# Reordering two steps: the eighth gelu and the state's high part on ScalarE, the fourth piece of the second feed-forward product and the second tile's products with the state on TensorE

## The reference, cut to what matters

```python
x = x + attention(layernorm(x))
x = x + ffn(layernorm(x))

# attention: xn is the normalized x, xx its difference to the token before
xk, xv, xr, xg = (xn + xx * maa for maa in (maa_k, maa_v, maa_r, maa_g))
r, k, v = xr @ Wr.T, xk @ Wk.T, xv @ Wv.T      # split by head
g = silu(xg @ Wg.T)
# in order over chunks of 64 tokens, for each head:
att = (r_c @ k_c) * w_mat                       # 64 x 64 weights
y_c = att @ v_c + (r_c @ state) * wb
state = ws * state + (k_c * wk) @ v_c
# then
out = (groupnorm_by_head(y) * gamma + beta) * g @ Wo.T

# ffn
D = gelu(fp16(xn2) @ W0.T + bias0)
E = fp16(D) @ W1.T + bias1
```

## Time and profile before

| what | value |
|---|---|
| median of 3 runs | 2086.19 us (2080.97 to 2089.77) |
| profiled execution, its own time | 2082.99 us |
| span of its trace | 2081.2 us |
| granted TensorE clock, mean | 0.995 of full speed |
| TensorE matmul busy | 96% of the span |
| VectorE busy | 84% |
| ScalarE busy | 62% |
| GpSimd busy | 16% |
| DMA, mean share of the 16 engines | 76% for the dynamic queue |

### The profile page before, as it was taken

One profiled execution on the slowest core, in us unless ns is written; L12 is line 12 of the kernel. 1 busy time (PEld: TensorE's weight loads), 2 busy tenths in 40 slices (PEclk: granted clock), 3 DMA queues, 4 the chain that ended last, 5 costly groups with the idle time before them and its releaser, 6 DMA issues.

```text
span 2081.2 us, 64752 instructions
## 1 busy us (share of the span) xinstructions
PE 2002.4 (96%) x27206; PEld 1421.4 (68%) x27206; DVE 1743.3 (84%) x3687; ACT 1294.1 (62%) x2081; POOL 333.1 (16%) x329
## 2 busy tenths in 40 slices
PE   5888999999999999999999999999999999999999
PEld 5767667677667667766666766666776676677666
DVE  7778889888889888888988888888888898888761
ACT  7866556666556576656667665656765666766452
POOL 1011111111111111111111111111111111111110
PEclk8999999999999999999999999999999999999999
DMA  6877677887777788777778877778887777887767
GB/s 213 203 199 211 199 224 230 241 248 217 216 231 222 233 249 239 206 223 230 221 239 249 226 209 221 224 229 249 243 219 214 229 226 236 245 243 199 215 236 264
DMA packets 428979, 471.97 MB, mean 227 GB/s; under 512 B 259600, under 2 KB 309392, under 8 KB 428688
## 3 DMA queue, kind: packets, MB, share of 16 engines
q1 hardware_dynamic: 427056, 467.64, 76.1%
q10 hardware_dynamic: 1632, 0.18, 0.1%
HBM read 316.21 MB, written 25.17 MB: 164 GB/s over the span
## 4 chain that ended last, share of the span: by engine, by line
PE 78%; SPq 5%; ACT 5%; DVE 4%; DMA 4%; issue 2%; POOL 0%; ACTq 0%; DVEq 0%
PE F L1132 18%; PE F L1068 16%; PE B L879 9%; PE B L1040 8%; PE sc L879 7%; PE YT L911 5%; PE YT L879 3%; PE YT L963 2%; DMA y<-ygT 2%; ACT hT L1766 2%; SPq L2025 2%; PE YT L982 2%; PE YT L1012 1%; PE sc L941 1%; PE F L836 1%
## 5 line engine op out<-in xcount | busy, mean ns | idle before, releaser
L1132 PE MATMUL F<-ring,hT 128*128 128x512 f16 x1984 | 468.0, 379 | 19.3 <-ACT hT L1766 18.8
L1068 PE MATMUL F<-xT,ring 128*128 128x256 f16 x3840 | 449.3, 273 | 5.6 <-ACT hT L1766 3.7
L1068 PEld LDWEIGHTS F<-xT,ring 128*128 128x128 f16 x3840 | 369.9, 98 | 65.3 <-issue 8.2
L1132 PEld LDWEIGHTS F<-ring,hT 128*128 128x128 f16 x1984 | 186.7, 98 | 224.9 <-ACT hT L1766 33.5
L879 PE MATMUL B<-mix,WT 128*128 128x256 f16 x2304 | 267.5, 273 | 0.3 <-DVE gT L1371 0.3
L1766 ACT ACTIVATE hT<-F,b,f_rho 128x256 f16<-128x256 f32 x480 | 244.0, 561 | 37.8 <-PE F L1068 37.8
L879 PEld LDWEIGHTS B<-mix,WT 128*128 128x128 f16 x2304 | 222.6, 98 | 33.6 <-DVE gT L1371 0.7
L276 DVE SCALAR_TENSOR_TENSOR mixf<-dx,maa,xnT 128x256 f32<-128x256 f32 x512 | 238.6, 527 | 0.1
L1969 POOL TENSOR_TENSOR Shl<-S,Shl 128x256 f16<-128x256 f32 x128 | 104.6, 817 | 723.3 <-ACT Shl L1723 723.3
L1717 ACT ACTIVATE att<-att 128x512 f16<-128x512 f32 x256 | 147.5, 624 | 110.3 <-DVE att L1332 110.3
L1723 ACT ACTIVATE Shl<-S 128x256 f16<-128x256 f32 x128 | 53.1, 415 | 224.1 <-PE YT L982 201.9
(11 more groups left out here) (196 smaller groups left out, 2993.5 us busy)
## 6 DMA issues: line engine op xcount, KB each, us to landing
ring<-w_dram SPq DMA_DIRECT2D x512, 512.0 KB, 4.7
kx<-kT SPq DMA_DIRECT2D x96, 256.0 KB, 3.7
rx<-rT SPq DMA_DIRECT2D x96, 256.0 KB, 4.3
xa<-in_L_attn_x SPq DMA_DIRECT2D x32, 512.0 KB, 7.7
vbd<-vN SPq DMA_DIRECT2D x256, 64.0 KB
x<-in_L_attn_x SPq DMA_DIRECT2D x32, 512.0 KB, 6.0
out<-x SPq DMA_DIRECT2D x31, 512.0 KB, 3.9
w_dram<-ring SPq DMA_DIRECT2D x20, 256.0 KB, 3.2
```

The costliest lines, as they stand in the source:

```text
L1068: mm = eng.matmul(up_place(f, j)[:, i * BT:(i + 1) * BT], ring[:, use % RING, i, a * C + kk * P:a * C + (kk + 1) * P], xT[:, :, kk, :], st ...
L1132: mm = eng.matmul(F[:, t, :], hT[:, k, rows(t)], ring[:, use % RING, i, a * C:(a + 1) * C], start=(k == 0 and a == 0), stop=(k == NH - 1 a ...
```

## The change

On ScalarE, in steady steps, the eighth gelu (number 7) is issued ahead of the high part of the state after chunk 1, and no longer behind it. On TensorE, in every step that has both attention and feed-forward (2 to 31), down 3 is issued between att_v(1) and from_state(1), and no longer behind from_state(1). No operation is added, removed or resized.

```diff
@@ pe_step
         if att_n:
             pe_att_v(eng, n, 1)
-            pe_from_state(eng, n, 1)
         if ff:
             pe_down(eng, n - 2, 3)
+        if att_n:
+            pe_from_state(eng, n, 1)
@@ act_steady
         if ahead:
             act_mix_hi(eng, n + 1, 1)
         act_gelu(eng, n, 6)
+        act_gelu(eng, n, 7)
         act_state_hi(eng, n, 1)
-        act_gelu(eng, n, 7)
         act_weights_hi(eng, n, 2)
```

## The result

| kernel | median (runs) | ratio to before, 95% interval |
|---|---|---|
| before | 2087.84 us (18) | |
| changed | 2091.95 us (2087.62 to 2100.08, 18) | 1.0028 (1.0016 to 1.0039) |
| changed, run again later | 2093.72 us (2088.94 to 2097.84, 12) | 1.0037 (1.0020 to 1.0053) |

The change costs 0.3%, some 6 us, against a forecast of 0.8%. One of the 18 runs of the kernel before took 4135 us, twice as long as all the others, and is left out of the ratio. The loss is real but lies within the 0.5% that I had called no change.

The account below looks back on a forecast made before the run. TensorE's list plus one hole a step at down 0 was taken as the bound. 2083.0 - 13 (gelu 7) + 28 (late join) + 4 (ring loads) = 2102 us, plus 1 for the median: 2103 us, range 2071 to 2120.

Parts of the forecast that it names:

- the absorbed lag: Rival: only 0.9 us of the lateness reaches the join of y's words; 2085 us, no change; chance 0.20.
- The hole of 0.94 us in each step: TensorE at down 0, waiting for gelu 7: 0.94 us a step from start to start, 27 us if all came back.
- What is late next: At att_v(1), TensorE would wait for VectorE's line 1351: 0.48 us a step becomes a new wait, 0.46 us is kept.
- Part 1: Gelu 7 ahead of the state's high part on ScalarE: 13 us gained, bounds 0 and 27 us.
- The lag of 1.73 us from from_state(1) to VectorE's y and row means: Down 3 ahead of from_state(1) makes VectorE's take of y and the row means 1.73 us later against TensorE.
- slack of 0.4 us: At V(0), the mix's low part has 2.1 us of slack, 0.4 left after the move; no cost.
- SP never waits in between, so all come later: SP's row from x's words to y's words: all 1.6 us later, bounds 1.2 and 1.73; +28 us at the join.
- The price of a late join: ScalarE's join of y's words to TensorE's up 6: 0.55 us of slack, then each microsecond late costs TensorE one.
- Ring loads, +4 us: SP's load for up 7, issued 1.6 us later, misses up 7 in some steps: +4 us, bounds 0 and 8.
- doesn't do what it says: Rival: gelu 7 waits elsewhere, so only down 3's move counts; 2115 us, chance 0.03.
- the worse case: Rival: the 0.46 us a step don't come and loads for up 5 to up 7 are late too; 2122 us, chance 0.10.
- part 2 alone: Only down 3 moved ahead of from_state(1) on TensorE, with no gain from gelu 7: 2115 us.

Follow-up runs that it names:

- gelu_alone: Only gelu 7 moved ahead of the state's high part, down 3 left in place, against the kernel before: 2081.57 us, ratio 0.9981.
- light_loads: Changed kernel with the two ring loads for up 3 and up 4 cut to a quarter: 2064.60 us, ratio 0.9892 to the kernel before.
- down_alone: Only down 3 moved ahead of from_state(1), gelu 7 left in place, against the kernel before: 2103.81 us, ratio 1.0087.
- split4_again: Second run: gelu 7 moved, half of down 3 ahead of att_v(1), half behind from_state(1), against the kernel before: 2075.89 us, ratio 0.9932.
- between4: Gelu 7 moved, half of down 3 between att_v(1) and from_state(1), half behind from_state(1), against the kernel before: 2085.36 us, ratio 0.9983.

## Why the prediction was right or wrong, point by point

- **The forecast, 2103 us, 0.8% slower: the sign is right, the size is not.** 0.3% is within the 0.5% to which I had given 0.20, against 0.61 for slower. The rival that came true is the absorbed lag (0.9 us left, +14 us). Its price was right, 13.4 us in the table; its 2085 us is 7 us too low.
- **The hole of 0.94 us in each step: nearly right.** 23.0 us came back in 28 steps, 0.82 us each. Taking it from start to start and not from the idle row was right: the row says 18.8 us.
- **What is late next: right in the place, too large in size.** TensorE now waits at att_v(1) for the line that reads kv, in step 28 by 0.17 us, and by 0.19 to 0.24 us a step from Wo(1) on (5.2 to 6.2 us in 28 steps) instead of 0.48. Two things made the difference: the hole was 0.82 and not 0.94 us, and VectorE's chain came 0.54 us earlier and not 0.46. Part 1 is therefore worth 17 to 18 us in the order, where I had 13. It isn't worth that in time: by itself it gave 4 to 5 us, and the trace of gelu_alone shows waits for issue and a lower clock behind them in place of most of the rest, two terms that the prediction put at nothing.
- **The lag of 1.73 us from from_state(1) to VectorE's y and row means: exactly right.** The row means end 9.79 us after K(0) instead of 8.05; the idle row of `dve_take_y(n, 1)` is 1.99 us where I said 1.9; ScalarE waits 2.05 us for the row means instead of 0.33. V(0) had its slack of 0.4 us and never waited for the mix.
- **The step that failed: "SP never waits in between, so all come later".** I took 1.6 us with 1.2 as the least. Measured, as the mean start after K(0) over steps 3 to 30: x's words 1.7 us later (14.90 instead of 13.22), rx 0.9, k 0.9, y's words 0.95 (25.59 instead of 24.64). The lag is lost in one place, the issue of the transpose of x's words, which takes 2.8 us instead of 3.7 (medians of 28: 2846 and 3726 ns), and lands in 4.7 instead of 5.5 us. Before, then changed:

```profile
L313 SPq DMA_TRANSPOSE att<-att x28: 3312/3726/4072, 243.7 to 1897.2; - x28
...
DMA to landing us min/median/max: 4.9/5.5/6.9
```

```profile
L313 SPq DMA_TRANSPOSE att<-att x28: 2279/2846/3510, 245.0 to 1913.3; - x28
...
DMA to landing us min/median/max: 4.6/4.7/6.4
```

  So the same SP issue isn't a fixed cost here, and a row of issues without a gap can have slack inside the issues. That it stretches while transfers ahead of it are worked off is shown for the two transposes behind it: with the two loads cut, that of y's words took 2.6 instead of 3.5 us and that of k 3.2 instead of 4.2 (medians, light_loads and changed kernel). For the transpose of x's words itself no run took its neighbours away, so there this cause is argued. I had written that sentence down ("fill it, so no row shows one") and then given such slack 0.13 us. That the changed kernel in both its traces, down_alone and light_loads show the same 3.6 us from x's words to rx (before: 4.4) makes it a property of the order, not chance.
- **The price of a late join (0.55 us of slack, then one to one): right.** Step 6 gives 8.47 us from join to up 6. The lateness was too large: the join waited 31 us in all where I expected 40 to 55, and the segment from up 5 to up 6 grew by 13 to 14 us where I had 28.
- **Ring loads, +4 us: right** (2.8 to 5.2 us at up 5 and up 7).
- **Not in the sum:** TensorE's waits for issue, 6 us more than before; the lower clock, 0.5 for 3.4 us behind one wait in the first trace, which costs 1.7 us, and in the second not at all; and a tenth of a microsecond in each step between att_v(1) and K(0) (60.99 instead of 60.89 in down_alone), 3 us.
- By the terms of the trace: -18 + 13.4 + 5 + 6 + 3 = +9 us (11 with the clock of the first trace), of the 15 us by which the 28 steps are longer in the first trace and the 11 us in the second; in the medians +6 us. What is left isn't assigned. The rule of the Trainium skill that I had named for the full lag (DMA: Bandwidth & Descriptors, on descriptors consumed in ring order) isn't contradicted; it says nothing on how long the issue ahead takes, and that was the point that decided.
- The chance of 0.03 for "doesn't do what it says" and the worse case (2122 us) didn't come; down_alone at 2104 us is what part 2 alone costs, where I had 2115.

## What to carry to other kernels

Two moves in one change have to be timed apart: here a good one (gelu 7, a wait taken out of the longest engine's list) carried a bad one (down 3, which made the only producer of a long chain through three engines and a DMA row 1.7 us later), and half the bad move in another place gave 0.65% instead of a loss of 0.3%. When a piece of filler work is moved, ask first what stands behind it on its own engine and which chain hangs on that; a full engine that stays full can still lose at the far end of the loop. A transfer's lateness is not passed on whole: look at how long the issues themselves take, and whether these times are longer than the same issue takes in a quieter stretch. And look at the granted clock behind a long wait of TensorE before you believe that the wait cost only its own length.

## What the runs showed of the hardware

TensorE can stand still for 1 to 3.3 us in the middle of a group of short matmuls with no semaphore open. The trace also records instruction transfers: 216 of 16 KB on one queue, one in 9.3 us on average. In all 48 such waits of 0.7 us or more from step 3 on, in twelve traces, one of them ended 1.1 to 1.7 us before the group went on, and the one before it had started 5 to 11 us earlier. The wait of 1.1 to 1.2 us at L1068 near 190 us, ahead of step 3, is another matter: it stands in every trace, and the last transfer lay some 10 us back. That the engine had run out of instructions is inferred from this coincidence and not tried by itself. The Trainium skill (Runtime: NRT & Kernel Launch, "Instruction fetch mechanics") says that instructions come in blocks of 16 KiB, 256 of them, while the block before is worked off, and that the cost of crossing a block is mostly hidden. The size agrees with the profile's row of 216 transfers and 3.54 MB; the hiding is seen only in part.

```profile
q8 instruction: 216, 3.54, 0.7%
```

The waits sum up to 1 to 5 us in four of the kernels and to 7 to 16 us in the others, and the longest stood in the same few steps in different kernels and runs (near 1270 and 1575 us of the span; where there were more, also near 655, 960 and 1880, each five steps from the next). I hadn't expected a cost that is tied to places in the program and that moves by more than the whole change is worth.

Such a wait can cost more than its length. Between 200 and 1970 us of the 14 traces the granted clock stood at its upper level (2.4 GHz) but for 13 stretches at 0.5 (1.2 GHz), twelve of 3.4 us and one of 6.8. Each began during a wait of TensorE of 1.5 to 3.3 us or less than 1 us behind it: 11 times a wait for issue, twice one for a ring load (1.8 us near 1324 us in the changed kernel, 1.75 us near 1005 us in split4_again). Other waits as long had none behind them (2.2 us in the kernel before, 2.4 in between4), so the price of one wait can't be foretold from its length here.
